# Index stage of a fused transformer kernel: eight of the sixteen heads summed on GpSimd instead of six

## The chip, the cores and the metric

One core of one Trainium2 chip runs the whole program as one launch. The metric is the device time of that launch in microseconds. A shorter time is better. A difference under 0.2% of the time (6 us) is taken as no change.

## What is computed

The program chains seven stages over 2048 tokens of width 256: a mixture of experts, attention, experts again, a feed-forward stage, the **index** stage, the sparse attention over the rows that it selected, and a feed-forward stage. The change touches the index stage alone. Its reference, cut to what matters:

```python
qi = hadamard((x @ wq_idx).reshape(B, S, Hi, Di))    # Hi = 16 heads, Di = 128
ki = hadamard(x @ wk_idx)
iw = x @ w_iw                                        # one weight for each token and head
logits = relu(einsum('bthd,bsd->bhts', qi, ki))
I = einsum('bth,bhts->bts', iw, logits)              # sum over the 16 heads
I = where(causal, I, NEG)
vals, idx = top_k(I, 32)
```

So for each query token and each key the sixteen relu results are multiplied by a weight of either sign and added up. Then the 32 largest sums of each row are searched.

## The kernel before, in words

Queries are handled in tiles of 128 tokens (partitions), tile 15 first, tile 0 last (`TILE_ORDER`). A tile `t` needs the keys 0 to 128(t+1). These are cut into **passes** of at most 1024 keys (`WIDE`): tiles 15 to 8 have two passes, tiles 7 to 0 have one, 24 in all. Ten passes are 1024 wide (the two of tile 15, the first ones of tiles 14 to 8, and tile 7's); the other fourteen have the widths 896, 768, 640, 512, 384, 256 and 128, each twice. A pass goes through the heads 0 to 15. The text calls a pass of 1024 keys wide, and the others narrow.

One head of one pass is a unit (`iunits`), and goes like this:

- TensorE makes the scores in one of four PSUM slots of two banks (`ibanks`, `IR = 4`; lines 35 to 37 are the three matmuls of a split fp32 product). `room(key)` makes it wait until the unit four places earlier has left its slot.
- ScalarE takes the relu, scaled by the absolute value of the weight (`iwa`). `relu(|w| x)` needs the sign of `w` afterwards (`iws`, which is +1 or -1).
- For a head in `VH` the relu stays in PSUM (line 1771). VectorE multiplies by the sign and adds to `Isc` in one instruction (line 1858; for head 0 lines 1861, 1864 and 1865). The PSUM slot is free when VectorE is done.
- For a head in `PH` the relu goes to one of three SBUF buffers `rlp` (`RL = 3`, line 1778), and the PSUM slot is free as soon as ScalarE is done. ScalarE then multiplies the buffer by the sign (`signed`, line 1747), and GpSimd adds the buffer to `part_sum` (line 1914 for the first two heads at once, line 1917 for the others). `PH` is (1, 3, 5, 7, 9, 11), so `VH` has ten heads, and the heads 12 to 15 and 0 are five `VH` heads in a row.

After head 15 VectorE waits for GpSimd's last sum and adds `part_sum` to `Isc` (line 1871). GpSimd has one `part_sum`, so its first instruction of the next pass waits for this addition.

VectorE also searches the previous tile: 11 steps (`topk_step`, lines 1844, 1846, 1848, each over the whole row of the tile before; tiles 3 to 0 have other steps) are spread over the units of the tile. At tiles 15, 11, 7 and 3 the four key/value products of a group of tiles and eight query products (`("q", d, pair)`) come first in the queue of every engine; ScalarE copies a query product to `qih` and VectorE makes its rest, `qil` (line 1884).

All queues are written out in program order. The semaphores are: `i_L` scores ready, `i_R` relu done, `i_sg` sign set, `i_B` GpSimd's count, `i_A` VectorE's count.

Of the kernel before, what the change touches and what calls it, by code (L numbers as in the profile page):

```python
# [9 lines left out]
ALU = mybir.AluOpType  # L10
# [29 lines left out]
def build(nc, a, out, stages=("moe0", "attn0", "moe1", "ffn0", "index1", "select1", "ffn1")):  # L40
# [13 lines left out]
    with ctx:  # L54
# [7 lines left out]
        def sb(name, shape, dt, c=None):  # L62
            return (c or ctx).enter_context(nc.sbuf_tensor(name, shape, dt))
# [70 lines left out]
        def ln_gpsimd(g, n):  # L134
            for c in range(NCH):
                ln_root(g, n, c)
# [21 lines left out]
        def ln_scalar(s, n, c):  # L158
            q = NCH * n + c
            for k in range(KD):  # L160
                s.wait_ge(ln_tr, KD * q + k + 1)
                s.copy(XTh[:, k, CH * c:CH * (c + 1)], ln_bank(c, k, n)).then_inc(ln_hi, 1)
# [23 lines left out]
        before = sb("before", [P, P], F32, moe_ctx)  # L186
# [891 lines left out]
        for kind_, u_, h_, r_ in STEPS:  # L1078
            for k_ in range({"K": 2, "P": 3, "M": u_ % NCH + 1, "R": 1, "F": 1, "G": 2}.get(kind_, 0)):
                key_ = kind_, u_, h_, r_, k_  # L1080
# [456 lines left out]
        RL = 3  # L1537
# [8 lines left out]
        iws = iw  # L1546
        Isc = sb("Isc", [P, 2, T], F32, i_ctx)
        rlp = sb("rlp", [P, RL, WIDE], F32, i_ctx)
        part_sum = sb("part_sum", [P, WIDE], F32, i_ctx)
# [17 lines left out]
                             "i_A i_k i_sg i_B i_xt").split())  # L1567
        i_kvd = [sem("i_kvd0"), sem("i_kvd1")]
        NTB = (NHI + 1 + 1) // 2
        PH = (1, 3, 5, 7, 9, 11)  # L1570
        VH = tuple(h for h in range(NHI) if h not in PH)
        IR = 4
        QP = NHI // 2

        def iunits(t):

            return [(h, lo, min(WIDE, (t + 1) * P - lo)) for lo in range(0, (t + 1) * P, WIDE) for h in range(NHI)]

        def passes(t):
            return -(-((t + 1) * P) // WIDE)  # L1580
# [7 lines left out]
        SCORED, PASSED, QUEUE = {}, {}, {}  # L1588
# [13 lines left out]
                inumber, iscored, ipassed = inumber + 1, iscored + 1, ipassed + 1  # L1602
        ITEMS = list(QUEUE)
        PER = len(VH) + (len(PH) > 0)

        def searches(t):
            return DENSE_STEPS if t < DENSE else TOPK_STEPS
# [4 lines left out]
        def counted(t, h, lo):  # L1612

            heads = PH if h in PH else VH
            return len(heads) * PASSED[t, lo] + heads.index(h)

        def added(t, h, lo):

            return PER * PASSED[t, lo] + VH.index(h) + 1

        def finished(t):

            return PER * (PASSED[t, (passes(t) - 1) * WIDE] + 1)

        def ibanks(key):
            at = 2 * (QUEUE[key] % IR)
            return ps[:, at:at + 2, :].rearrange("p b s -> p (b s)")
# [12 lines left out]
        def index_tensor(pe, n):  # L1640
# [28 lines left out]
            def room(key):  # L1669
                if QUEUE[key] >= IR:  # L1670
# [3 lines left out]
                    elif before[0] == "q":  # L1674
                        pe.wait_ge(i_ql, QP * before[1] + before[2] + 1)
                    elif before[1] in PH:
                        pe.wait_ge(i_R, SCORED[before] + 1)
# [43 lines left out]
        def index_scalar(s, n):  # L1721
            k0 = LNA[n]

            def turned(first, last):
                for m in range(first, last):
                    hs = slice(2 * m, min(2 * m + 2, NHI + 1))
                    size = (hs.stop - hs.start) * KD * DI
                    s.wait_ge(i_t, m + 1)
                    s.copy(wih[:, hs], ps[:, 4 + m % 4, 0:size]).then_inc(i_th, 1)

            s.wait_ge(i_c, 64)
            s.copy(ikv_h[:], ikv_raw[:]).then_inc(i_rh, 1)
            ln_scalar(s, k0, 0)
            ln_scalar(s, k0, 1)
            turned(0, 4)
            ln_scalar(s, k0, 2)
            turned(4, NTB)
            ln_scalar(s, k0, 3)
            for c in range(NCH):
                s.wait_ge(i_ki, c + 1)  # L1740
                s.copy(KIh[:, CH * c:CH * (c + 1)], ps[:, 2 + c % 2, :]).then_inc(i_kh, 1)
            before = None

            def signed(t, h, lo, w):
                at = rlp[:, counted(t, h, lo) % RL, 0:w]
                s.wait_ge(i_R, SCORED[t, h, lo] + 1)
                s.activation(at, at, ACT.Copy, scale=iws[:, t, h:h + 1]).then_inc(i_sg, 1)  # L1747

            for d in range(NCH):
                c = NCH - 1 - d  # L1750
                for t in reversed(range(CT * c, CT * (c + 1))):
                    p = TILES - 1 - t
                    o = ibanks(("kv", t, 0))
                    s.wait_ge(i_kv, p + 1)
                    if p >= 2:
                        s.wait_ge(i_kvd[p % 2], 16 * (p // 2))
                    s.copy(iw[:, t, :], o[:, 2 * P:KVI])
                    s.copy(kvs[:, p % 2, :], o[:, 0:2 * P]).then_inc(i_kve, 1)
                for pair in range(QP):
                    s.wait_ge(i_q, QP * d + pair + 1)  # L1760
                    if d >= 1 and pair == 0:
                        s.wait_ge(i_L, SCORED[CT * (c + 1), NHI - 1, (passes(CT * (c + 1)) - 1) * WIDE] + 1)
                    s.copy(qih[:, 2 * pair:2 * pair + 2, :].rearrange("p h t -> p (h t)"), ibanks(("q", d, pair))).then_inc(i_qh, 1)
                s.wait_ge(i_iw, 4 * (d + 1))
                for t in reversed(range(CT * c, CT * (c + 1))):
                    for h, lo, w in iunits(t):
                        key = (t, h, lo)
                        o = ibanks(key)[:, 0:w]
                        s.wait_ge(i_L, SCORED[key] + 1)
                        if h in VH:  # L1770
                            s.activation(o, o, ACT.Relu, scale=iwa[:, t, h:h + 1]).then_inc(i_R, 1)  # L1771
                            if before:
                                signed(*before)
                            before = None
                        else:
                            m = counted(t, h, lo)
                            s.wait_ge(i_B, max(m - RL + 1, 0))
                            s.activation(rlp[:, m % RL, 0:w], o, ACT.Relu, scale=iwa[:, t, h:h + 1]).then_inc(i_R, 1)  # L1778
                            before = t, h, lo, w

        def index_vector(v, n):
            k0 = LNA[n]
# [68 lines left out]
            def scores(t, h, lo, w):  # L1851
                acc = Isc[:, t % 2, lo:lo + w]
                if h in VH:
                    o = ibanks((t, h, lo))
                    v.wait_ge(i_R, SCORED[t, h, lo] + 1)
                    if h > 0:
                        v.wait_ge(i_A, added(t, h, lo) - 1)
                        i = v.scalar_tensor_tensor(out=acc, in0=o[:, 0:w], scalar=iws[:, t, h:h + 1], in1=acc,  # L1858
                                                   op0=ALU.mult, op1=ALU.add)
                    elif lo + w < (t + 1) * P:  # L1860
                        i = v.tensor_scalar(acc, o[:, 0:w], iws[:, t, h:h + 1], None, ALU.mult)
                    else:
                        if w > P:
                            v.tensor_scalar(acc[:, 0:w - P], o[:, 0:w - P], iws[:, t, h:h + 1], None, ALU.mult)
                        i = v.scalar_tensor_tensor(out=acc[:, w - P:w], in0=o[:, w - P:w], scalar=iws[:, t, h:h + 1],
                                                   in1=imask[:], op0=ALU.mult, op1=ALU.add)
                    i.then_inc(i_A, 1)
                if h == NHI - 1 and PH:
                    v.wait_ge(i_A, added(t, VH[-1], lo))
                    v.wait_ge(i_B, len(PH) * (PASSED[t, lo] + 1))  # L1870
                    v.tensor_tensor(acc, acc, part_sum[:, 0:w], ALU.add).then_inc(i_A, 1)

            for d in range(NCH):
# [30 lines left out]
        def index_gpsimd(g, n):  # L1904
            ln_gpsimd(g, LNA[n])
            for t in TILE_ORDER:
                for h, lo, w in iunits(t):
                    if h in PH[1:]:
                        m = counted(t, h, lo)
                        at = rlp[:, m % RL, 0:w]  # L1910
                        g.wait_ge(i_sg, m + 1)
                        if h == PH[1]:
                            g.wait_ge(i_A, PER * PASSED[t, lo])
                            g.tensor_tensor(part_sum[:, 0:w], rlp[:, (m - 1) % RL, 0:w], at, ALU.add).then_inc(i_B, 2)  # L1914
                        else:
                            g.wait_ge(i_B, m)
                            g.tensor_tensor(part_sum[:, 0:w], part_sum[:, 0:w], at, ALU.add).then_inc(i_B, 1)  # L1917


# [506 lines left out]
```

## Time and profile before

| what | us |
|---|---|
| median of three runs | 2947.57 (2947.53 to 2949.59) |
| the profiled execution, its own time | 2954.38 |
| its span, first to last instruction | 2952.6 |
| scoring part of the index stage within the span (tile 15's first VectorE operation to the last addition) | 1571.3 to 2150.6 |
| mean granted TensorE clock of the span | 0.946 of 2.4 GHz |

The profile counts time from the span's start. Its views name engines as PE (TensorE), DVE (VectorE), ACT (ScalarE) and POOL (GpSimd). A row of a group says line, engine, operation, output and input, shape, count, then the busy time, the mean duration of one in ns, and how long the engine sat idle just before. Durations of successive instructions of one engine can overlap a little: ScalarE's next relu starts about 0.1 us before the last one is recorded as ended, and a matmul of 512 columns is recorded as 0.39 us while the next one starts 0.23 us after it.

### The profile page before, as it was taken

How to read it: one execution, taken by the hardware profiler on the slowest of the kernel's cores; microseconds unless marked ns; L12 is line 12 of the kernel's file. 1: busy time of each engine (PE TensorE's matmuls, PEld its weight loads, DVE VectorE, ACT ScalarE, POOL GpSimd, SP SyncE). 2: the span in 40 equal slices, each digit the busy share in tenths (PEclk: the TensorE clock that was granted, in tenths of full speed). 3: DMA queues.
4: the chain of work that ended last, by engine and by line, in shares of the span. 5: the costliest groups of instructions: out<-in, count | busy, mean ns of one | idle time of the engine just before them, and what ended most of it. 6: DMA issues, size and time to landing. Idle time of an engine off the chain costs nothing. (4 is left out here: it accounts for less than half of the span.)

```text
span 2952.6 us, 42059 instructions
## 1 busy us (share of the span) xinstructions
PE 2561.3 (87%) x14687; PEld 1967.1 (67%) x14687; DVE 1816.7 (62%) x3482; ACT 1492.5 (51%) x2918; POOL 1039.1 (35%) x943
## 2 busy tenths in 40 slices
PE   4957999999999996797979889898868988888798
PEld 4845555555556554676867777676768877776587
DVE  7556865865766754645455997989835444445443
ACT  3435557457556555342227876767644433434232
POOL 2642212212202201452223432424246565657232
PEclk9978999999999996898989999999989999999899
DMA  4241000000000003223010000000033232323200
GB/s 156 85 137 50 8 9 23 17 19 19 11 23 8 11 1 110 67 80 101 29 40 4 1 6 2 1 8 1 8 108 90 83 88 85 93 79 97 89 2 29
DMA packets 70266, 138.63 MB, mean 47 GB/s; under 512 B 16816, under 2 KB 38024, under 8 KB 68912
## 3 DMA queue, kind: packets, MB, share of 16 engines
q0 software_dynamic: 26336, 73.01, 8.3%
q1 hardware_dynamic: 43728, 62.95, 6.4%
q8 instruction: 125, 2.05, 0.3%
q14 instruction: 77, 0.63, 0.1%
HBM read 114.71 MB, written 20.81 MB: 46 GB/s over the span
## 5 line engine op out<-in xcount | busy, mean ns | idle before, releaser
L1437 ACT ACTIVATE PT<-ps 128x512 f32<-128x512 f32 (+3 forms) x640 | 313.4, 534 | 283.1 <-PE ps L1190 147.2
L2260 POOL DMA_INDIRECT KV<-kv_scratch,sidx x384 | 367.9, 958 | 238.7 <-PE ps L2107 115.3
L1303 DVE TENSOR_REDUCE xn<-ps 128x1 f32<-128x512 f32 (+3 forms) x640 | 342.4, 601 | 61.4 <-PE ps L1167 45.5
L35 PE MATMUL ps<-KIh,qih 128*128 128x512 f32 (+2 forms) x640 | 250.8, 392 | 66.0 <-DVE Isc L1858 39.7
L1858 DVE SCALAR_TENSOR_TENSOR Isc<-ps,iw,Isc 128x1024 f32<-128x1024 f32 (+7 forms) x216 | 208.6, 966 | 54.5 <-ACT ps L1771 48.4
L36 PE MATMUL ps<-KIl,qih 128*128 128x512 f32 (+2 forms) x640 | 242.0, 378 | 0.0
L37 PE MATMUL ps<-KIh,qil 128*128 128x512 f32 (+2 forms) x640 | 241.8, 378 | 0.0
L2182 ACT ACTIVATE sP<-sP,snm 128x128 f32<-128x128 f32 (+2 forms) x256 | 110.4, 432 | 251.0 <-DVE snm L2245 251.0
L1187 PE MATMUL ps<-qB,KB 128*128 128x512 f32 (+2 forms) x640 | 234.1, 366 | 0.0
L1771 ACT ACTIVATE ps<-ps,iwa 128x1024 f32<-128x1024 f32 (+7 forms) x240 | 198.2, 858 | 62.6 <-PE ps L37 62.1
L35 PEld LDWEIGHTS ps<-KIh,qih 128*128 128x128 f32 x640 | 126.3, 197 | 113.0 <-issue 91.8
L1470 POOL TENSOR_TENSOR rr<-rb 128x512 f32<-128x512 f32 x64 | 82.3, 1285 | 325.7 <-DVE rb L1295 322.3
L1473 POOL TENSOR_TENSOR qB<-rr,qA 64x512 fp32r<-64x512 f32 x64 | 81.7, 1277 | 323.8 <-ACT qB L1427 323.7
L1917 POOL TENSOR_TENSOR part_sum<-part_sum,rlp 128x1024 f32<-128x1024 f32 (+7 forms) x96 | 168.4, 1755 | 61.2 <-ACT rlp L1747 61.2
L1914 POOL TENSOR_TENSOR part_sum<-rlp 128x1024 f32<-128x1024 f32 (+7 forms) x24 | 42.2, 1757 | 352.5 <-ACT rlp L1747 281.3
L858 POOL TENSOR_TENSOR fyl<-fy,fyh 128x512 fp32r<-128x512 f32 x64 | 84.4, 1318 | 215.8 <-ACT fyh L769 215.8
L1200 PE MATMUL ps<-PT,VG 128*32 128x512 f32 (+3 forms) x1280 | 150.0, 540 | 3.8 <-ACT Osb L1441 3.5
L37 PEld LDWEIGHTS ps<-KIh,qil 128*128 128x128 f32 x640 | 126.4, 197 | 20.8
L36 PEld LDWEIGHTS ps<-KIl,qih 128*128 128x128 f32 x640 | 126.8, 198 | 19.5
L1186 PE MATMUL ps<-qA,XTh 128*128 128x512 f32 (+2 forms) x320 | 133.7, 418 | 5.1 <-DMA qA<-mrow 4.9
L1186 PE MATMUL ps<-qA,XTl 128*128 128x512 f32 (+2 forms) x320 | 136.0, 425 | 0.0
L1778 ACT ACTIVATE rlp<-ps,iwa 128x1024 f32<-128x1024 f32 (+7 forms) x144 | 125.5, 872 | 19.5 <-PE ps L37 18.8
(362 smaller groups left out, 6963.3 us busy)
## 6 DMA issues: line engine op xcount, KB each, us to landing
cs<-in_rope SPq DMA_DIRECT2D x20, 512.0 KB, 4.2
ycomb<-y_rows SPq DMA_DIRECT2D x16, 512.0 KB, 5.0
w1raw<-in_w SPq DMA_DIRECT2D x14, 512.0 KB, 6.7
KV<-kv_scratch,sidx POOLq DMA_INDIRECT x384
xn_rows<-xnr SPq DMA_DIRECT2D x8, 512.0 KB, 4.9
whr<-in_whead SPq DMA_DIRECT2D x16, 256.0 KB, 2.8
w2raw<-in_w SPq DMA_DIRECT2D x14, 256.0 KB, 7.0
wir<-in_wi SPq DMA_DIRECT2D x1, 2176.0 KB, 7.9
```

Source lines behind the costliest of these rows:

```text
L35: pe.matmul(out, lhs[0], rhs[0], start=start, stop=False)
L36: pe.matmul(out, lhs[0], rhs[1], start=False, stop=False)
L37: return pe.matmul(out, lhs[1], rhs[0], start=False, stop=stop)
L1186: pe.matmul(o[:, mm_lo:CH], KA[hh][:, j * P:(j + 1) * P], qA[:, par, hh, mm_lo:CH], start=True, stop=False)
L1187: i = pe.matmul(o[:, mm_lo:CH], KB[:, j * P:(j + 1) * P], qB[:, par, hh, mm_lo:CH], start=False, stop=j < CT * c)
L1200: i = pe.matmul(ps[2 * HD * hh:2 * HD * (hh + 1), AV_BANK, lo:CH], VG[:, j, hh, :], PT[:, ROUND[u, j] % 2, hh, lo:CH], start=j == 0, stop= ...
L1303: v.tensor_reduce(mp[:, CT * h + r, k:k + 1], o[:, 0:end], AX_X, ALU.max).then_inc(a_free, 1)
L1437: s.activation(PT[:, rnd % 2, hh, lo:CH], ps[:, ST_BANKS[e % 3], lo:CH], ACT.Exp, scale=SCALE).then_inc(a_exp, 1)
L1771: s.activation(o, o, ACT.Relu, scale=iwa[:, t, h:h + 1]).then_inc(i_R, 1)
L1858: i = v.scalar_tensor_tensor(out=acc, in0=o[:, 0:w], scalar=iws[:, t, h:h + 1], in1=acc, op0=ALU.mult, op1=ALU.add)
L1917: g.tensor_tensor(part_sum[:, 0:w], part_sum[:, 0:w], at, ALU.add).then_inc(i_B, 1)
L2260: g.indirect_dma_start(KV[:, BG * (k % RB) + m, :], None, a["kv_scratch"], bass.IndirectOffsetOnAxis(sidx[:, t % 2, at:at + 1], 0)).then_i ...
```

## The change

`PH` becomes (1, 2, 4, 5, 7, 8, 10, 11), so `VH` is (0, 3, 6, 9, 12, 13, 14, 15). ScalarE still multiplies by the sign for the four heads in `SH`, (2, 5, 8, 11). For the other four (1, 4, 7, 10) GpSimd does it: for head 1 with a `tensor_scalar` that writes `part_sum`, for the others with a `tensor_scalar` in place in `rlp`, followed by the addition. There are still three `rlp` buffers, one `part_sum` and four PSUM slots. TensorE's queue has the same instructions in the same order.

```diff
-        PH = (1, 3, 5, 7, 9, 11)
+        PH = (1, 2, 4, 5, 7, 8, 10, 11)
+        SH = (2, 5, 8, 11)
...
+        PKEYS = [key_ for key_ in ITEMS if key_ in SCORED and key_[1] in PH]
...
+        def signed_by_act(t, h, lo):
+            return len(SH) * PASSED[t, lo] + SH.index(h) + 1
+
+        def summed(t, h, lo):
+
+            heads = PH[:PH.index(h) + 1]
+            return (2 * len(PH) - 1 - len(SH)) * PASSED[t, lo] + 2 * len(heads) - 1 - sum(x in SH for x in heads)
...
                         else:
+                            if before:
+                                signed(*before)
                             m = counted(t, h, lo)
-                            s.wait_ge(i_B, max(m - RL + 1, 0))
+                            if m >= RL:
+                                s.wait_ge(i_B, summed(*PKEYS[m - RL]))
                             s.activation(rlp[:, m % RL, 0:w], o, ACT.Relu, scale=iwa[:, t, h:h + 1]).then_inc(i_R, 1)
-                            before = t, h, lo, w
+                            before = (t, h, lo, w) if h in SH else None
...
-                    v.wait_ge(i_B, len(PH) * (PASSED[t, lo] + 1))
+                    v.wait_ge(i_B, summed(t, PH[-1], lo))
...
-                    if h in PH[1:]:
+                    if h in PH:
                         m = counted(t, h, lo)
-                        at = rlp[:, m % RL, 0:w]
-                        g.wait_ge(i_sg, m + 1)
-                        if h == PH[1]:
+                        at, sign = rlp[:, m % RL, 0:w], iws[:, t, h:h + 1]
+                        if h == PH[0]:
+                            g.wait_ge(i_R, SCORED[t, h, lo] + 1)
                             g.wait_ge(i_A, PER * PASSED[t, lo])
-                            g.tensor_tensor(part_sum[:, 0:w], rlp[:, (m - 1) % RL, 0:w], at, ALU.add).then_inc(i_B, 2)
+                            g.tensor_scalar(part_sum[:, 0:w], at, sign, None, ALU.mult).then_inc(i_B, 1)
                         else:
-                            g.wait_ge(i_B, m)
+                            if h in SH:
+                                g.wait_ge(i_sg, signed_by_act(t, h, lo))
+                            else:
+                                g.wait_ge(i_R, SCORED[t, h, lo] + 1)
+                                g.tensor_scalar(at, at, sign, None, ALU.mult).then_inc(i_B, 1)
+                            g.wait_ge(i_B, summed(t, h, lo) - 1)
                             g.tensor_tensor(part_sum[:, 0:w], part_sum[:, 0:w], at, ALU.add).then_inc(i_B, 1)
```

GpSimd's queue for one pass of 1024 keys, with the semaphores that each instruction waits for. Before:

```order
L1914 TENSOR_TENSOR part_sum<-rlp 128x1024 [waits i_A,i_sg]
L1917 TENSOR_TENSOR part_sum<-part_sum,rlp 128x1024 [waits i_B,i_sg] x4
```

With the change:

```order
L1927 TENSOR_SCALAR part_sum<-rlp,iw 128x1024 [waits i_A,i_R]
L1935 TENSOR_TENSOR part_sum<-part_sum,rlp 128x1024 [waits i_B,i_sg]
L1933 TENSOR_SCALAR rlp<-rlp,iw 128x1024 [waits i_R]
L1935 TENSOR_TENSOR part_sum<-part_sum,rlp 128x1024 [waits i_B]
L1935 TENSOR_TENSOR part_sum<-part_sum,rlp 128x1024 [waits i_B,i_sg]
L1933 TENSOR_SCALAR rlp<-rlp,iw 128x1024 [waits i_R]
L1935 TENSOR_TENSOR part_sum<-part_sum,rlp 128x1024 [waits i_B]
L1935 TENSOR_TENSOR part_sum<-part_sum,rlp 128x1024 [waits i_B,i_sg]
L1933 TENSOR_SCALAR rlp<-rlp,iw 128x1024 [waits i_R]
L1935 TENSOR_TENSOR part_sum<-part_sum,rlp 128x1024 [waits i_B]
L1935 TENSOR_TENSOR part_sum<-part_sum,rlp 128x1024 [waits i_B,i_sg]
```

Five additions become seven, and four multiplications by the sign are new.

VectorE's queue in the first pass of tile 14, from head 0 to the addition of `part_sum`. Before (a row with x2 or x3 is that many heads):

```order
L1861 TENSOR_SCALAR Isc<-ps,iw 128x1024
L1858 SCALAR_TENSOR_TENSOR Isc<-ps,iw,Isc 128x1024
L1844 MAX v<-Isc 128x8
L1858 SCALAR_TENSOR_TENSOR Isc<-ps,iw,Isc 128x1024
L1846 MAX_INDEX xn<-v,Isc 128x8
L1858 SCALAR_TENSOR_TENSOR Isc<-ps,iw,Isc 128x1024 x2
L1848 MATCH_REPLACE Isc<-v,Isc 128x2048
L1858 SCALAR_TENSOR_TENSOR Isc<-ps,iw,Isc 128x1024
L1844 MAX v<-Isc 128x8
L1858 SCALAR_TENSOR_TENSOR Isc<-ps,iw,Isc 128x1024 x3
L1846 MAX_INDEX xn<-v,Isc 128x8
```

With the change:

```order
L1874 TENSOR_SCALAR Isc<-ps,iw 128x1024
L1857 MAX v8<-Isc 128x8
L1871 SCALAR_TENSOR_TENSOR Isc<-ps,iw,Isc 128x1024
L1859 MAX_INDEX xn<-v8,Isc 128x8
L1871 SCALAR_TENSOR_TENSOR Isc<-ps,iw,Isc 128x1024
L1861 MATCH_REPLACE Isc<-v8,Isc 128x2048
L1871 SCALAR_TENSOR_TENSOR Isc<-ps,iw,Isc 128x1024
L1857 MAX v8<-Isc 128x8
L1871 SCALAR_TENSOR_TENSOR Isc<-ps,iw,Isc 128x1024 x3
L1859 MAX_INDEX xn<-v8,Isc 128x8
```

In both, head 15's SCALAR_TENSOR_TENSOR and the addition of `part_sum` follow. Two of the ten head operations are gone, both before head 12; the search steps stay where they were. ScalarE's queue loses two of its six sign operations of each pass, and its relu of a `PH` head now follows another one directly.

## Rows read from the trace of the kernel before

**Rows 1.** The page: span, and busy time of each engine.

```profile
span 2952.6 us, 42059 instructions
PE 2561.3 (87%) x14687; PEld 1967.1 (67%) x14687; DVE 1816.7 (62%) x3482; ACT 1492.5 (51%) x2918; POOL 1039.1 (35%) x943
```

**Rows 2.** Windows, one a pass: length, PE, PEld, DVE, ACT, POOL busy, clock, DMA.

```profile
1598.20:1622.00 23.80, 22.85 (x98) 17.76 (x97) 14.09 (x14) 22.61 (x23) 12.02 (x5) 1.00 0.00 1
1622.00:1647.90 25.90, 22.98 (x96) 17.64 (x95) 24.75 (x21) 23.54 (x24) 12.03 (x5) 0.98 0.00 1
1671.80:1699.90 28.10, 22.75 (x100) 17.73 (x98) 26.45 (x23) 23.38 (x24) 12.06 (x5) 1.00 0.00 1
1699.90:1721.50 21.60, 18.12 (x95) 14.93 (x94) 21.15 (x21) 17.20 (x21) 9.26 (x5) 1.00 0.00 1
1881.30:1908.30 27.00, 21.45 (x93) 16.69 (x91) 23.61 (x23) 22.39 (x26) 12.02 (x5) 0.97 0.00 1
1908.30:1921.40 13.10, 10.11 (x51) 8.88 (x52) 12.65 (x22) 8.55 (x20) 3.65 (x5) 0.81 0.00 1
2011.00:2036.40 25.40, 20.31 (x97) 16.80 (x96) 25.16 (x31) 20.82 (x23) 10.65 (x5) 1.00 0.00 1
```

**Rows 3.** Waits from 1570 to 2155 us: total, times, longest.

```profile
ACT ps L1771 <- PE ps L37: 62.1, 66, 3.4
DVE Isc L1858 <- ACT ps L1771: 48.4, 59, 1.8
PE ps L35 <- DVE Isc L1858: 43.2, 52, 2.2
```

**Rows 4.** Groups of VectorE, shapes apart, 1570 to 2155 us.

```profile
L1858 DVE SCALAR_TENSOR_TENSOR Isc<-ps,iw,Isc 128x1024 f32<-128x1024 f32 x90 | 115.1, 1279 | 44.4 <-ACT ps L1771 41.9
...
L1858 DVE SCALAR_TENSOR_TENSOR Isc<-ps,iw,Isc 128x896 f32<-128x896 f32 x18 | 20.5, 1138 | 0.7 <-ACT ps L1771 0.3
...
L1858 DVE SCALAR_TENSOR_TENSOR Isc<-ps,iw,Isc 128x128 f32<-128x128 f32 x18 | 6.2, 343 | 1.2 <-ACT ps L1771 0.6
```

**Rows 5.** Timeline of ScalarE in tile 8's first pass: start, duration, idle before.

```profile
1929.20 1.08 ACT L1771 ACTIVATE ps<-ps,iwa 128x1024 f32<-128x1024 f32 x1
1930.19 1.16 ACT L1747 ACTIVATE rlp<-rlp,iw 128x1024 f32<-128x1024 f32 x1
1931.24 1.12 ACT L1778 ACTIVATE rlp<-ps,iwa 128x1024 f32<-128x1024 f32 x1
1932.23 1.10 ACT L1771 ACTIVATE ps<-ps,iwa 128x1024 f32<-128x1024 f32 x1
...
1938.30 1.12 ACT L1771 ACTIVATE ps<-ps,iwa 128x1024 f32<-128x1024 f32 x1
```

**Rows 6.** Timeline of TensorE in tile 15.

```profile
1597.66 0.39 PE L37 MATMUL ps<-KIh,qil 128*128 128x512 f32 x1
1597.89 0.40 PE L35 MATMUL ps<-KIh,qih 128*128 128x512 f32 x1
```

**Rows 7.** Timeline of VectorE at the end of tile 8's first pass.

```profile
1941.50 2.67 DVE L1858 SCALAR_TENSOR_TENSOR Isc<-ps,iw,Isc 128x1024 f32<-128x1024 f32 x2 [0.76 <-ACT ps L1771]
...
1944.16 1.49 DVE L1846 FIND_INDEX8 xn<-v,Isc 128x8 uint32<-128x1280 f32 x1
1945.56 1.26 DVE L1858 SCALAR_TENSOR_TENSOR Isc<-ps,iw,Isc 128x1024 f32<-128x1024 f32 x1
1946.86 1.22 DVE L1871 TENSOR_TENSOR Isc<-Isc,part_sum 128x1024 f32<-128x1024 f32 x1
```

**Rows 8.** Groups of GpSimd's additions and ScalarE's signs, index stage.

```profile
L1917 POOL TENSOR_TENSOR part_sum<-part_sum,rlp 128x1024 f32<-128x1024 f32 x40 | 96.1, 2403 | 25.4 <-ACT rlp L1747 25.4
...
L1917 POOL TENSOR_TENSOR part_sum<-part_sum,rlp 128x896 f32<-128x896 f32 x8 | 17.0, 2130 | 4.7 <-ACT rlp L1747 4.7
...
L1747 ACT ACTIVATE rlp<-rlp,iw 128x1024 f32<-128x1024 f32 (+7 forms) x144 | 130.8, 908 | 0.0
```

**Rows 9.** Groups of other GpSimd work in the whole span.

```profile
L132 POOL TENSOR_TENSOR rstd<-veps,mhalf 128x4 f32<-128x4 f32 x24 | 27.2, 1133 | 2.0
...
L1451 POOL MEMSET tmpq<- 128x1024 f32 x1 | 1.0, 953 | 0.0
```

## The prediction

> **What bounds the kernel now.** The page [rows 1] shows only that no engine fills the span: VectorE 62%, GpSimd 35%. The change lies in the scoring part of the index stage, 579 of 2953 us, so I read that part pass by pass. In the windows [rows 2] compare each engine's busy time with the length. In the narrow passes VectorE is full: 21.15 of 21.6 us in tile 13's second pass, 12.65 of 13.1 in tile 9's, 25.16 of 25.4 in tile 6's. There, every VectorE instruction that goes is time that goes. In the wide passes nobody is full: tile 9's first has VectorE at 23.61 and ScalarE at 22.39 of 27.0 us; tile 15's second has VectorE at 14.09 and ScalarE at 22.61 of 23.8. The waits [rows 3] say the same: TensorE waits for VectorE to free a PSUM slot, VectorE waits for ScalarE, ScalarE for TensorE, each 40 to 60 us in all; no long one has GpSimd as the cause.
>
> A wide pass has two halves. In **heads 1 to 11** ScalarE sets the pace: relu, sign, relu follow each other without a gap, and two heads take 1929.20 to 1932.23, 3.03 us [rows 5], while TensorE would need 2 x 6 matmuls x 0.23 = 2.8 us [rows 6]. In **heads 12 to 15** VectorE does: in tile 8's first pass, which begins at 1921.4 [rows 2], head 12's relu starts at 1938.30, 16.9 us in [rows 5]; then VectorE has heads 13 and 14 (2.67), a search step (1.49), head 15 (1.26) and the addition of `part_sum` (1.22), until 1948.1 [rows 7]: 9.8 us from the relu's start.
>
> **The change, part by part.**
>
> *VectorE, two heads fewer in each pass.* One costs 1.279 us at 1024 keys, 1.138 at 896, 0.343 at 128 [rows 4]. The fourteen narrow passes are two of each width from 128 to 896; the duration grows evenly with the width, so the mean is (1.138 + 0.343) / 2 = 0.74 and the 28 instructions are 20.7 us. VectorE is full there, so nearly all counts; I take off 2 us for the narrow passes of tiles 3 and 4, beside query products and key/value products that TensorE sets. **-19 us.**
>
> *ScalarE, two signs fewer.* In all 144 signs are 130.8 us [rows 8], a third goes, 44 us. In the narrow passes this is hidden behind VectorE, which stays the longer: tile 13's second pass has 21.15 against 17.20 [rows 2]. In the wide passes it moves the pace of heads 1 to 11 from ScalarE to TensorE: three heads are now four ScalarE operations of 1.01 us, 4.05, against 18 matmuls, 4.2 us. Eleven heads at 1.4 instead of 1.52 are 1.3 us less, at most. The end of the pass, from head 12 on, is VectorE's and has the same instructions. In tile 8 TensorE alone would bring head 12 about 1.0 us sooner. I take 1.0 for each of the first passes of tiles 7 to 11. Tile 14's I put at 0.8, since it is only 25.9 us long. Tiles 13 and 12 are longer, because VectorE with a 2048 or 1792 wide search is nearly full there (26.45 of 28.1 [rows 2]): the two heads are 2.56 us, of which I count 2.1 and 2.5. Tile 15's two passes: nothing, see the next part. 5.0 + 0.8 + 4.6 = **-10.4 us.**
>
> *GpSimd, more work.* Before, five additions of 2.403 us, 12.0 us in a wide pass [rows 2, 8]; now seven, 16.8 us, and four multiplications. The trace has no GpSimd multiplication by a column of scalars at these widths. From below: a memset of 128x1024 takes 0.953 us [rows 9], which only writes. From above: the addition, two inputs and one output, 2.403. A multiplication reads one and writes one. Half of an addition for the one input it reads is 1.20, and it lies just above the memset; I take c = **1.25 us** and keep 0.95 to 2.4 for the range. Each instruction waits for the semaphore of the one before; the pair of line 130 and line 132 shows 2.0 us over 24 such waits [rows 9], 0.08 us. So GpSimd's round in a wide pass is 11 instructions, 4 c + 16.8 + 0.9, then VectorE's addition of 1.2 and a signal of 0.1, before the single `part_sum` is free: 4 c + 19.0 = 24.0 us. That is above the 23.8 of tile 15's second pass and below the 25.9 to 28.1 of the others [rows 2]. So tile 15 gains nothing, and the others may shrink as far as the sum above has them. At 896 keys an addition is 2.130 and the round about 21.5, just under VectorE's. One more wait is in it: ScalarE's relu into a buffer waits for the sum three `PH` heads back. Head 11's waits for head 7's: 3 c + 4 x 2.4 + 0.6 = 14.0 us after GpSimd's start, which in tile 8 is 0.9 us into the pass. Everything behind it in ScalarE's queue, heads 12 to 15, waits too, and VectorE with them. Head 11's relu would be ready about 14.5 us into the pass, so the wait is some 0.4 us. I charge **+1.5 us** for the wide passes.
>
> The Trainium skill ("GPSIMD Engine Reference", section 4.1, Engine selection) speaks against elementwise work on GpSimd: two-input operations about twice as slow as on VectorE, one-input ones roughly at line rate. The first half agrees with the trace, 2.403 against 1.22 us for an addition [rows 7, 8]. By the second half c would be near 1.0, and the sum, an estimate, some 2 us better. No run here shows that half yet.
>
> *Sum:* -19 - 10.4 + 1.5 = -28. TensorE's queue, the DMAs and every other stage are unchanged: nothing. Against the profiled execution (2954.4, which stands 6.8 above the median) that is 2926; against the median of 2947.6 it is **2919.5 us**.
>
> **The rivals.**
>
> *A. GpSimd's multiplication costs about what an addition does, and GpSimd's round becomes the bound.* For it: it is the same engine, with a fixed share for each element, and in-place work behind a semaphore. Against: one input less. With c = 2.4 the round is 28.6 us in a wide pass. The passes of before are 23.8 to 28.1 [rows 2]; over the ten I count a mean of 26.7, so ten of them lose 1.9 each, 19 us. At 896 and 768 keys the rounds would be 25.4 and 22.3, 1 us over what stands there; the other narrow passes keep their gain, about 10 us. Together +11: **2959 us**. It is slower than before from c = 2.2 up.
>
> *B. In between, c around 1.9.* The round of a wide pass is 26.6: the wide passes as a whole gain nothing, head 11's relu comes 1.9 us later, and the narrow ones give 15 to 17. **2932 us.**
>
> *C. VectorE's time does not come back in full.* The eight heads left are unevenly placed: three in heads 1 to 11, five in a row from head 12. TensorE can only be four units ahead, so what VectorE saves before head 12 may turn into waiting for ScalarE, also in passes where it is full now. Then the narrow passes give half, 10 us, and the wide ones 5 to 8: **2931 us**. Against it: the search steps are spread over all heads, and in tile 13's second pass heads 1 to 11 leave VectorE three heads and four steps of about 2 us, 11.2 us, with ScalarE at 15 operations of 0.8, 12.0, and ahead by some heads.
>
> *D. VectorE gives all of it.* Both heads gone count everywhere but in tile 15, and c is near 1.0: 48 instructions less four of tile 15, about 41 us, **2907 us**.
>
> **How the numbers follow.** Forecast (c up to 1.6, loss small) 0.57; D 0.08; C 0.13; B 0.08; A 0.11; 0.03 for a mix that ends near zero. A measurement of this kernel tells 0.2%, 6 us, from no change. Faster by more than that: forecast, D, C and nearly all of B, 0.85. Slower by more: most of A, 0.09. Within: the rest, 0.06. The range leaves out D's best end and the upper part of A: 2908 to 2942.
>
> **What would show it.** Right: a multiplication row of GpSimd at 1.0 to 1.5 us for 1024 keys; VectorE still full in the narrow passes, tile 13's second near 19.6 us instead of 21.6; wide passes of 24 to 26 us with TensorE's matmuls 0.23 apart through heads 1 to 11; GpSimd at 20 to 22 us of them. Wrong: a multiplication of 2 us and more; VectorE's addition of `part_sum` waiting for GpSimd in most passes; ScalarE's relu into `rlp` waiting for GpSimd by over a microsecond; narrow passes in which VectorE sits idle waiting for ScalarE.

## The result, and the profile after

The change makes the kernel slower: 3022.69 us median (3017.36 to 3025.36) against 2948.58 before, a ratio of 1.0243, 95% interval 1.0225 to 1.0261. The forecast was 2919.5. Even the slower rival, 2959, is far below what was measured. The two profiled executions, from which all rows come, are 63.0 us apart (3017.36 and 2954.38).

The page of the changed kernel, span and busy time of each engine, against [rows 1]:

```profile
span 3015.1 us, 42104 instructions
PE 2582.9 (86%) x14687; PEld 1977.9 (66%) x14687; DVE 1775.6 (59%) x3434; ACT 1463.0 (49%) x2870; POOL 1322.6 (44%) x1087
```

VectorE lost 41 us of work and ScalarE 29.5 (its sign operations by themselves add up to 86.0 us in place of 130.8), and GpSimd gained 283.5 us. The forecast amounts to some 169 us of new work there: the mean addition of before was 1.755 us, so 48 more are 84 us, and 96 multiplications at half of that another 84.

The windows of the changed kernel show passes that answer to those of [rows 2]: the second pass of tile 15, the first of tile 14, both of tile 13, both of tile 9, and tile 6's. The columns are the length, then PE, PEld, DVE, ACT and POOL busy, the granted clock, DMA share and GB/s:

```profile
1603.40:1633.80 30.40, 24.79 (x96) 18.76 (x96) 11.52 (x12) 21.29 (x21) 28.08 (x11) 0.94 0.00 1
1633.80:1664.20 30.40, 25.43 (x95) 19.55 (x96) 22.42 (x19) 19.41 (x19) 28.05 (x11) 0.89 0.00 0
1691.60:1724.00 32.40, 24.73 (x98) 18.82 (x97) 24.10 (x21) 21.01 (x21) 28.07 (x11) 0.93 0.00 1
1724.00:1748.20 24.20, 21.00 (x97) 17.12 (x96) 19.40 (x21) 16.73 (x20) 21.64 (x11) 0.88 0.00 1
1921.80:1953.00 31.20, 22.22 (x92) 16.77 (x90) 20.80 (x19) 20.89 (x23) 28.00 (x11) 0.93 0.00 1
1953.00:1965.00 12.00, 10.39 (x51) 9.44 (x52) 11.76 (x21) 7.84 (x18) 8.83 (x11) 0.77 0.01 2
2064.90:2093.60 28.70, 21.60 (x95) 18.05 (x96) 23.57 (x29) 17.99 (x20) 24.86 (x11) 0.94 0.00 1
```

Where 23.8, 25.9, 28.1 and 27.0 us stood, there are 30.4, 30.4, 32.4 and 31.2, and in each GpSimd works 28 us in place of 12. Of the narrow passes only the second ones of tiles 10, 9 and 8 gain (tile 9's from 13.1 to 12.0, where VectorE is still full); the last passes, of the same three widths in tiles 2, 1 and 0, are 0.4 to 1.7 us longer. The granted clock is lower than before, 0.88 to 0.94 in most of them, behind TensorE's longer waits. What this lower clock costs by itself no run here shows. Over the scoring part, adding up from one addition of `part_sum` to the next, the ten wide passes went from 318.0 to 366.3 us, and the fourteen narrow ones from 261.3 to 279.9.

Groups of GpSimd in the changed kernel, shapes apart: line, operation, tiles, shape, count, then busy us, mean ns of one, and the idle time before:

```profile
L1935 POOL TENSOR_TENSOR part_sum<-part_sum,rlp 128x1024 f32<-128x1024 f32 x70 | 167.0, 2386 | 13.5 <-ACT rlp L1757 6.3
L1933 POOL TENSOR_SCALAR rlp<-rlp,iw 128x1024 f32<-128x1024 f32 x30 | 85.6, 2852 | 2.8 <-ACT rlp L1791 2.8
...
L1927 POOL TENSOR_SCALAR part_sum<-rlp,iw 128x1024 f32<-128x1024 f32 x10 | 28.5, 2850 | 118.0 <-ACT rlp L1791 110.2 <-DVE Isc L1884 7.8
```

The multiplication takes **2.85 us**, more than the addition it was bounded by (2.403 [rows 8]). In place or into `part_sum`, it is the same.

How that reaches VectorE is to be seen in the first pass of tile 8, which begins at 1965.0. Timeline of ScalarE in the changed kernel (start, duration; in brackets the idle time before and its releaser):

```profile
1977.52 1.12 ACT L1791 ACTIVATE rlp<-ps,iwa 128x1024 f32<-128x1024 f32 x1 [1.81 <-POOL part_sum L1935]
1978.53 1.08 ACT L1781 ACTIVATE ps<-ps,iwa 128x1024 f32<-128x1024 f32 x1
...
1985.33 1.11 ACT L1791 ACTIVATE rlp<-ps,iwa 128x1024 f32<-128x1024 f32 x1 [3.64 <-POOL part_sum L1935]
1986.34 1.08 ACT L1781 ACTIVATE ps<-ps,iwa 128x1024 f32<-128x1024 f32 x1
```

and of VectorE, just after:

```profile
1987.45 1.28 DVE L1871 SCALAR_TENSOR_TENSOR Isc<-ps,iw,Isc 128x1024 f32<-128x1024 f32 x1 [5.12 <-ACT ps L1781]
...
1995.61 1.23 DVE L1884 TENSOR_TENSOR Isc<-Isc,part_sum 128x1024 f32<-128x1024 f32 x1 [0.79 <-POOL part_sum L1935]
```

Head 11's relu (1985.33) waits 3.64 us until GpSimd has emptied a buffer. Head 12's relu stands behind it and starts at 1986.34, 21.3 us into the pass, where it had been 16.9 us. VectorE, idle for 5.12 us, then does the same end of the pass as before. The whole shift of the pass is 5.1 us: 4.4 by head 12's relu, and the rest by GpSimd's own last sum, which comes out at almost the same place: VectorE's addition waits 0.79 us for it.

The waits of the changed kernel from 1570 to 2235 us (total, times, longest), against [rows 3]:

```profile
DVE Isc L1871 <- ACT ps L1781: 152.8, 79, 6.8
...
ACT rlp L1791 <- POOL part_sum L1935: 76.2, 34, 3.9
...
PE ps L35 <- DVE Isc L1871: 50.6, 65, 2.2
```

A wait that did not appear among those of before, ScalarE for GpSimd, is 76.2 us, and VectorE's wait for ScalarE has tripled from 48.4.

### The profile page after: what moved, and what is told of

Its sections match the earlier page's. It is cut to its first block and busy times, and to the rows that moved or that the text cites. A ratio compares the mean times of both kernels' runs of the same rounds, so it can differ in the third digit from the quotient of the medians.

```text
span 3015.1 us, 42104 instructions
## 1 busy us (share of the span) xinstructions
PE 2582.9 (86%) x14687; PEld 1977.9 (66%) x14687; DVE 1775.6 (59%) x3434; ACT 1463.0 (49%) x2870; POOL 1322.6 (44%) x1087
## 5 line engine op out<-in xcount | busy, mean ns | idle before, releaser
L35 PE MATMUL ps<-KIh,qih 128*128 128x512 f32 (+2 forms) x640 | 260.1, 406 | 110.6 <-DVE Isc L1871 46.2
L1935 POOL TENSOR_TENSOR part_sum<-part_sum,rlp 128x1024 f32<-128x1024 f32 (+7 forms) x168 | 293.1, 1745 | 28.3 <-ACT rlp L1757 9.9
L1871 DVE SCALAR_TENSOR_TENSOR Isc<-ps,iw,Isc 128x1024 f32<-128x1024 f32 (+7 forms) x168 | 162.5, 967 | 155.7 <-ACT ps L1781 152.8
L36 PE MATMUL ps<-KIl,qih 128*128 128x512 f32 (+2 forms) x640 | 248.8, 389 | 0.0
L37 PE MATMUL ps<-KIh,qil 128*128 128x512 f32 (+2 forms) x640 | 248.1, 388 | 0.0
L1791 ACT ACTIVATE rlp<-ps,iwa 128x1024 f32<-128x1024 f32 (+7 forms) x192 | 165.3, 867 | 143.5 <-POOL part_sum L1935 76.2
L1781 ACT ACTIVATE ps<-ps,iwa 128x1024 f32<-128x1024 f32 (+7 forms) x192 | 155.5, 842 | 37.0 <-PE ps L37 36.7
L1933 POOL TENSOR_SCALAR rlp<-rlp,iw 128x1024 f32<-128x1024 f32 (+7 forms) x72 | 151.4, 2103 | 10.1 <-ACT rlp L1791 10.0
```

The source lines that it names most:

```text
L35: pe.matmul(out, lhs[0], rhs[0], start=start, stop=False)
L36: pe.matmul(out, lhs[0], rhs[1], start=False, stop=False)
L37: return pe.matmul(out, lhs[1], rhs[0], start=False, stop=stop)
```

## The experiments

Twelve kernels ran. The medians are each beside runs of the kernel before on the same chip, whose medians were 2950.8 to 2952.4 us. Where two runs from different chips are set against each other below, each is taken by its distance from its own runs of before.

**1. Eight heads, all signs on ScalarE.** The kernel before with the change's `PH`, and a pending sign set before the next relu into a buffer:

```diff
-        PH = (1, 3, 5, 7, 9, 11)
+        PH = (1, 2, 4, 5, 7, 8, 10, 11)
...
+                            if before:
+                                signed(*before)
                             m = counted(t, h, lo)
                             s.wait_ge(i_B, max(m - RL + 1, 0))
```

> Eight heads on GpSimd as in the change, but ScalarE sets all eight signs and GpSimd only adds (7 additions a pass). Theory M (the multiplication, 2.85 us at 1024 keys, makes GpSimd's round 4 x 2.85 + 19.0 = 30.4 us and so the bound): the round falls to about 18.9 us, GpSimd no longer holds anybody, the wide passes come down from 31 us to 26 to 28 (ScalarE has 24 operations of 1.01 us), the narrow ones to VectorE's time; 2935 to 2955 us. Rival W (the uneven placing of the eight heads, with more heads for three rlp buffers, is what costs): stays at 2990 to 3020.

Measured: 2991.7 us, ratio 1.0135 (1.0115 to 1.0155). Theory M's 2935 to 2955 fails, and the value is at W's lower end. GpSimd is no longer in anybody's way (16.8 us busy in a wide pass), but the wide passes are 26.0 to 31.4 us (tiles 11 and 7, which hold the query products, aside), with ScalarE busy 24.6 to 26.0 of them. From head 1 on, before head 12's relu, ScalarE now has 11 relus and 7 signs, and in tile 8 that relu starts 19.5 us into the pass in place of 16.9; the end of the pass hangs on it. So eight heads with eight signs on ScalarE is no reference for "GpSimd without multiplications": it puts another load in its place. The waits say so: VectorE waits 127.9 us for ScalarE.

```profile
DVE Isc L1860 <- ACT ps L1771: 127.9, 84, 4.5
```

**2. Six heads, three signs on GpSimd.** The change with

```diff
-        PH = (1, 2, 4, 5, 7, 8, 10, 11)
-        SH = (2, 5, 8, 11)
+        PH = (1, 3, 5, 7, 9, 11)
+        SH = (3, 7, 11)
```

> The six heads of before on GpSimd, but GpSimd sets the sign of three of them (1, 5, 9) itself. Theory M: its round in a wide pass is 3 x 2.85 + 5 x 2.4 + 0.6 + 1.3 = 22.5 us, under the passes of before, so nothing is lost and ScalarE's three signs less give a little: 2935 to 2950 us. A rival by which the multiplication disturbs VectorE or ScalarE (shared memory access) rather than fills GpSimd: three quarters of the loss, 2990 to 3005.

Measured: 2953.0 us, ratio 1.0003 (0.9994 to 1.0013): no difference. The multiplication costs 2.854 us here too:

```profile
L1933 POOL TENSOR_SCALAR rlp<-rlp,iw 128x1024 f32<-128x1024 f32 x20 | 57.1, 2854 | 0.0
```

The rival (the multiplication disturbs the other engines) is out: 72 of them, three quarters of the change's, cost nothing in sum while GpSimd's work of 20.5 us fits in the pass. What was also expected, a small gain by ScalarE's 72 signs less, did not come.

**3. The constant 1.0 instead of the column of signs.**

```diff
-                            g.tensor_scalar(part_sum[:, 0:w], at, sign, None, ALU.mult).then_inc(i_B, 1)
+                            g.tensor_scalar(part_sum[:, 0:w], at, 1.0, None, ALU.mult).then_inc(i_B, 1)
...
-                                g.tensor_scalar(at, at, sign, None, ALU.mult).then_inc(i_B, 1)
+                                g.tensor_scalar(at, at, 1.0, None, ALU.mult).then_inc(i_B, 1)
```

> The change, but GpSimd multiplies by the constant 1.0 instead of by the column of signs, so the signs of heads 1, 4, 7 and 10 are left out. If the column of scalars is what makes the multiplication dear, its row falls to 1.0 to 1.5 us and the time to 2915 to 2930; if a GpSimd tensor_scalar costs 2.85 us by itself, both stay: 2.85 us and 3015 to 3030.

Measured: 3020.6 us, ratio 1.0235. The row hardly falls:

```profile
L1933 POOL TENSOR_SCALAR rlp<-rlp 128x1024 f32<-128x1024 f32 x30 | 83.2, 2774 | 1.5 <-ACT rlp L1791 1.5
```

This kernel leaves four signs out. The column is not the price; GpSimd's `tensor_scalar` is.

**4. The sign by a tensor_tensor.**

```diff
-                                g.tensor_scalar(at, at, sign, None, ALU.mult).then_inc(i_B, 1)
+                                g.tensor_tensor(at, at, sign.to_broadcast([P, w]), ALU.mult).then_inc(i_B, 1)
```

and the same for head 1.

> The change, but the sign is multiplied with a tensor_tensor whose second input is the sign column read again for each key. If it costs what the additions do, 2.40 us: round of 4 x 2.4 + 19.0 = 28.6 us, 1.8 us less in each wide pass and a little less in the narrow ones: 2990 to 3000 us. If the column is slow to read, 2.8 us and more: 3015 and above.

Measured: 2983.6 us, ratio 1.0098 (1.0072 to 1.0123), below what was expected, since the row is cheaper than an addition:

```profile
L1933 POOL TENSOR_TENSOR rlp<-rlp,iw 128x1024 f32<-128x1024 f32 x30 | 56.8, 1895 | 2.6 <-ACT rlp L1791 2.6
```

The same computation in another operation gives back 43 of the 74 us. But with c = 1.9 the prediction's rival B had said 2932, so something else is missing as well, and runs 5 to 7 took it to be the placing of the heads.

The trace of this run shows what is missing. Its ten wide passes are still 24 us longer in all than before, and yet VectorE's addition waits for GpSimd only in tile 15 (twice, 2.0 us in all). Tile 8's first pass begins at 1941.6; GpSimd's first two operations, ScalarE's relus of heads 11 and 12, and VectorE's end of the pass:

```profile
1942.46 1.89 POOL L1927 TENSOR_TENSOR part_sum<-rlp,iw 128x1024 f32<-128x1024 f32 x1 [3.36 <-ACT rlp L1791]
1946.30 2.41 POOL L1935 TENSOR_TENSOR part_sum<-part_sum,rlp 128x1024 f32<-128x1024 f32 x1 [1.95 <-ACT rlp L1757]
...
1960.03 1.11 ACT L1791 ACTIVATE rlp<-ps,iwa 128x1024 f32<-128x1024 f32 x1 [2.72 <-POOL part_sum L1935]
1961.04 1.08 ACT L1781 ACTIVATE ps<-ps,iwa 128x1024 f32<-128x1024 f32 x1
...
1969.56 1.23 DVE L1884 TENSOR_TENSOR Isc<-Isc,part_sum 128x1024 f32<-128x1024 f32 x1
```

Head 12's relu starts 19.4 us into the pass, 2.5 later than before; the pass is 29.2 us, 2.5 longer; and the addition of `part_sum` waits for nothing. So here the whole loss of the pass comes through the wait of head 11's relu for a buffer, and none through GpSimd's last sum. No run had a fourth buffer, which would have tested this directly.

**5 to 7. The eight heads spread over the pass.** Run 5 is the kernel of run 1 with the first line, run 6 the change and run 7 the kernel of run 4 with both:

```diff
-        PH = (1, 2, 4, 5, 7, 8, 10, 11)
+        PH = (1, 3, 5, 7, 9, 10, 12, 14)
-        SH = (2, 5, 8, 11)
+        SH = (3, 7, 10, 14)
```

> As the run with eight heads and all signs on ScalarE (2991.7 us), but the eight heads are spread: 1, 3, 5, 7, 9, 10, 12, 14, so VectorE has 0, 2, 4, 6, 8, 11, 13, 15 instead of 0, 3, 6, 9, 12, 13, 14, 15. Work of each engine is the same. Theory P (placing: VectorE idles through heads 1 to 11 and then has five heads in a row, with TensorE never more than four units ahead): 2935 to 2955 us. Rival S (ScalarE's 24 operations a pass are the bound wherever the heads lie): stays at 2980 to 2995.

> The change itself with the heads spread as 1, 3, 5, 7, 9, 10, 12, 14, ScalarE signing 3, 7, 10, 14 and GpSimd 1, 5, 9, 12 with its tensor_scalar. Both causes: GpSimd's round of 30.4 us remains the bound of the wide passes, so little of the loss comes back, and its last sum now comes after head 14: 3000 to 3025 us. If placing alone made the loss: 2950 to 2965.

> Spread heads and the cheap multiplication (tensor_tensor with the column read again, 1.895 us): GpSimd's round is 4 x 1.9 + 19.0 = 26.6 us in a wide pass, about the mean of before (26.7), ScalarE has 20 operations. If placing and multiplication were the two causes, both are gone: 2925 to 2950 us. If eight heads on GpSimd cost something else too: 2965 and above.

Measured: 2975.5 us, 1.0090 (1.0061 to 1.0119); 3063.6 us, 1.0380 (1.0363 to 1.0397); 3014.7 us, 1.0219 (1.0202 to 1.0236). Run 5 lies between its two theories, 16 us faster than run 1; 6 and 7 are 37 and 31 us slower than the same kernels with the early heads, and run 6 lies outside both of its ranges. The theory that an even placing brings the loss back falls for the kernels in which GpSimd multiplies. The waits of run 6, from 1570 to 2235 us (its scoring part ends at 2263), show what takes its place:

```profile
DVE Isc L1884 <- POOL part_sum L1935: 110.6, 20, 6.9
...
PE ps L35 <- DVE Isc L1878: 88.9, 12, 8.3
```

With a head as late as 14, GpSimd's last sum comes after VectorE is through, VectorE waits with all that is queued behind it, and then TensorE waits for head 0's slot. In run 5, whose GpSimd only adds, VectorE's wait for the sum is 33.4 us. Early heads make ScalarE wait for buffers, late heads make VectorE wait for the sum. An evenly loaded VectorE was not tested apart from this by these runs.

**8. Seven heads, 13 among them.** The kernel of run 4 with

```diff
-        PH = (1, 2, 4, 5, 7, 8, 10, 11)
-        SH = (2, 5, 8, 11)
+        PH = (1, 3, 5, 7, 9, 11, 13)
+        SH = (3, 7, 11, 13)
```

> Seven heads, 1, 3, 5, 7, 9, 11, 13; ScalarE signs 3, 7, 11 and 13, GpSimd signs 1, 5 and 9 with the cheap tensor_tensor. The head taken from VectorE lies among the five in a row that held the end of each pass. GpSimd's round: 3 x 1.9 + 6 x 2.4 + 0.7 + 1.3 = 22.1 us, below the passes. VectorE loses one head a pass (24 x 0.97 = 23 us): 2920 to 2935 us. If the one that ends last is no longer VectorE there: 2945 to 2955.

Measured: 2943.5 us, ratio 0.9970 (0.9959 to 0.9980), faster than before by a little, between the two expected ranges. The narrow passes sum to 251.1 us against 261.3, the wide ones to 321.7 against 318.0.

**9. The change without its four multiplications.** GpSimd adds the first two buffers and then the others (the signs of heads 1, 4, 7 and 10 are missing), everything else is the change:

```diff
-                            g.tensor_scalar(part_sum[:, 0:w], at, sign, None, ALU.mult).then_inc(i_B, 1)
...
-                                g.tensor_scalar(at, at, sign, None, ALU.mult).then_inc(i_B, 1)
+                            if h == PH[1]:
+                                g.tensor_tensor(part_sum[:, 0:w], rlp[:, (m - 1) % RL, 0:w], at, ALU.add).then_inc(i_B, 2)
+                                continue
```

> The change with GpSimd's four multiplications left out (the signs of heads 1, 4, 7 and 10 are missing); heads, placing, ScalarE's 20 operations and seven additions as in the change. Theory H (a wide pass is the time until head 12's relu plus some 9.8 us of VectorE work; in the change head 11's relu waits for head 7's sum, 3 c + 4 x 2.4 + 0.6 us after GpSimd's start, 18.8 us with c = 2.85): with c = 0 that wait is gone, TensorE sets heads 1 to 11, wide passes of 25 to 26.5 us, narrow ones at VectorE's time: 2912 to 2930 us. Rival P (the uneven placing costs by itself, 2960 to 2985 us whatever GpSimd does).

Measured: 2938.1 us, ratio 0.9960 (0.9941 to 0.9979). This is the run that parts the loss in two. The change is 74 us above its runs of before and this kernel 13 below its own: the multiplications cost 87 us, more than the whole loss. Whether they do it by head 11's wait, as theory H has it, or by GpSimd's whole round, this run can't tell, since it takes both away; run 4 shows head 11's wait alone at work, and in the change's tile 8 the two came out within 0.8 us of each other. But 2938 is above H's 2912 to 2930, so a part of the forecast gain is missing even where GpSimd has no multiplication.

Part of what is missing is this kernel's own. GpSimd's first instruction now takes two buffers at once and can't begin before head 2's sign is set, so it frees head 1's buffer late, and head 5's relu waits for it: 1.41 us in tile 8, 1.66 each in tiles 11 and 7, 11.7 us in ten waits.

```profile
1919.35 1.12 ACT L1791 ACTIVATE rlp<-ps,iwa 128x1024 f32<-128x1024 f32 x1 [1.41 <-POOL part_sum L1933]
```

In the timeline of VectorE in tile 5's pass (768 keys, 23.4 us before, 23.5 here) the place shows:

```profile
2032.28 1.09 DVE L1857 MAX8 v<-Isc 128x8 f32<-128x896 f32 x1
2035.08 1.02 DVE L1871 SCALAR_TENSOR_TENSOR Isc<-ps,iw,Isc 128x768 f32<-128x768 f32 x1 [1.71 <-ACT ps L1781]
...
2043.24 1.02 DVE L1871 SCALAR_TENSOR_TENSOR Isc<-ps,iw,Isc 128x768 f32<-128x768 f32 x1 [0.60 <-ACT ps L1781]
```

VectorE has done head 3 and its search steps and stands idle for 1.71 us until head 6 arrives; head 13 waits 0.60 us, because ScalarE sets head 11's sign between the relus of 12 and 13. The windows of the same kernel for that pass and for tile 13's second (21.6 us before):

```profile
1697.00:1718.20 21.20, 19.80 (x98) 16.00 (x97) 19.40 (x19) 16.39 (x20) 12.94 (x7) 0.95 0.01 1
...
2025.70:2049.20 23.50, 19.94 (x97) 16.88 (x96) 20.85 (x29) 16.38 (x20) 12.90 (x7) 0.85 0.00 1
```

VectorE is busy 19.40 of 21.2 and 20.85 of 23.5: it lost the two heads' work and got idle time for most of it.

In tile 5's pass the clock has a share in this. TensorE had stood idle for head 0's slot, and then made the scores of heads 4 to 6 at the lower of its two levels, 1.2 GHz (granted clock 0.50); the 5.6 us at the same place of the pass before had 0.70:

```profile
2028.22 0.77 PE L35 MATMUL ps<-KIh,qih 128*128 128x512 f32 x1 [2.22 <-DVE Isc L1878]
```

The windows, first of this run, then of the kernel before:

```profile
2028.20:2033.80 5.60, 5.58 (x17) 4.74 (x18) 5.11 (x7) 1.80 (x2) 3.39 (x2) 0.50 0.00 0
2038.90:2044.50 5.60, 5.58 (x22) 4.80 (x23) 5.57 (x8) 3.24 (x4) 1.84 (x1) 0.70 0.02 3
```

How much of the 1.71 us is the placing and how much the clock is not shown. From 1571 to 2135 us the mean granted clock is 0.96 in both kernels.

**10. The same with later heads.** The kernel of run 9, without multiplications, with

```diff
-        PH = (1, 2, 4, 5, 7, 8, 10, 11)
-        SH = (2, 5, 8, 11)
+        PH = (1, 3, 5, 6, 8, 10, 11, 13)
+        SH = (3, 6, 10, 13)
```

> As the run before, without multiplications, with heads 1, 3, 5, 6, 8, 10, 11, 13 on GpSimd (ScalarE signs 3, 6, 10, 13; the signs of the others are missing), so only 12, 14, 15 and 0 stand at the end of a pass on VectorE. Theory H: the end of a wide pass is one head (1.28 us) shorter, unless VectorE waits for GpSimd's sum of head 13: 2905 to 2930 us. If late heads are what hurt in the spread runs (VectorE's addition waits for GpSimd's last sum): 2935 to 2960.

Measured: 2937.7 us, ratio 0.9966 (0.9952 to 0.9981): the same as run 9, in the second range and not in theory H's. The reason that was given for the second range is not what the trace shows: VectorE's addition waits only 5.7 us in all for GpSimd's last sum. One head fewer at the end of the pass brings nothing in sum; in exchange ScalarE waits for buffers again:

```profile
ACT rlp L1791 <- POOL part_sum L1933: 27.1, 21, 1.7
```

**11. Seven heads, signs on ScalarE.** The kernel before with

```diff
-        PH = (1, 3, 5, 7, 9, 11)
+        PH = (1, 3, 5, 7, 9, 11, 13)
```

> Seven heads, 1, 3, 5, 7, 9, 11, 13, all seven signs on ScalarE, so 23 of its operations a pass. Theory H: head 12's relu is as late as before (six signs ahead of it, as before), the end is one head shorter, narrow passes gain VectorE's one head: 2930 to 2945 us. If GpSimd's signing is what made the seven heads of the earlier run (2943.5 us) faster than before: 2950 to 2965.

Measured: 2940.9 us, ratio 0.9969 (0.9959 to 0.9980), as theory H has it. It is as fast as run 8, whose GpSimd sets three signs: moving these three signs to GpSimd is worth nothing either way, moving the one head is.

**12. Seven heads without a late one.** The kernel of run 8 with

```diff
-        PH = (1, 3, 5, 7, 9, 11, 13)
-        SH = (3, 7, 11, 13)
+        PH = (1, 3, 5, 7, 9, 11, 12)
+        SH = (3, 7, 11, 12)
```

> Seven heads, 1, 3, 5, 7, 9, 11, 12, GpSimd signing 1, 5 and 9 by tensor_tensor, ScalarE 3, 7, 11, 12. Against 1, 3, 5, 7, 9, 11, 13 (2943.5 us, where VectorE's addition waited 18.7 us for GpSimd's last sum) the last sum comes one head sooner: that wait mostly goes: 2925 to 2940 us. If it does not set the pace: 2940 to 2950.

Measured: 2952.7 us, ratio 1.0004 (0.9993 to 1.0015): 11 us slower than run 8, where up to 18 us faster had been expected, and outside both ranges. The wait of VectorE's addition for GpSimd in run 8 was this:

```profile
DVE Isc L1884 <- POOL part_sum L1935: 18.7, 15, 2.4
```

In run 12 it is 8.8 us, so it did shrink, but VectorE waits 63.5 us for ScalarE instead of 50.3. So that wait did not set the pace. Why head 12 is a worse choice than head 13 was not followed further.

## Why the prediction was wrong

**The change to GpSimd's round: the step that failed, by its size.** "From above: the addition, two inputs and one output, 2.403": this upper bound was an argument (one input fewer cannot cost more), not a measurement, and it is false on this engine. The multiplication takes 2.85 us, 1.6 more than the 1.25 taken. At this c the formulas behind it come close. The round, 4 c + 19.0, gives 30.4 us at 2.85; tile 15's second and tile 14's first pass are 30.4, the first passes of tiles 13 to 8 without query products 31.3 to 32.4. The wait of head 11's relu, 3 c + 4 x 2.4 + 0.6 after GpSimd's start, gives 18.8; in tile 8 GpSimd started at 0.9 and the relu at 20.3 us, 19.4 later. The 0.6 too little are in ScalarE's order: head 2's sign comes only after head 3's relu, so GpSimd's first addition waits 0.97 us.

**The same formula had a second fault, which c = 2.85 nearly hides.** GpSimd's first addition needs head 2's sign, and so starts 4.7 us into tile 8's first pass in the change and in run 4 alike. A first multiplication of 2.85 us fills most of the time until then; in run 4, with 1.9, GpSimd stands idle for 1.95 before the addition, and head 11's relu comes 17.6 us after GpSimd's start where the formula gives 15.9. From the rows of both runs: GpSimd's first addition ends at 7.1, then come two multiplications, three additions and their waits (7.5), so head 11's relu is at 14.6 + 2 c, which gives 20.3 and 18.4, as measured. With the forecast's own c of 1.25 this is an estimate of 17.1, not 14.9, and head 12's relu would be at 18.1, later than the 16.9 of before, where a gain of 1.0 was counted. No run has a multiplication of that length, but the time lies 13 us under before without any (run 9) and 31 above it at 1.9 (run 4). So "the wait is some 0.4 us" and the charge of 1.5 us were too small by themselves, and the forecast of -28 would probably have failed with the right c too. Rival B, 2932, missed run 4's 2984 by the same step.

**Rival A** had the mechanism, the bound and the direction, but c = 2.4 as its end and a chance of 0.11. Its sum of 2959 would be short even with the right c: wide passes of 30.4 to 32.4 in place of 28.6 (and the longer ones of tiles 11 and 7) give 48 us instead of 19, and the narrow passes, which it let keep about 10 us, lost 18.6. In tile 12's second pass, 640 keys, GpSimd is busy for 18.4 us and VectorE for 17.5, so GpSimd is the longer one there too.

**The skill's rule.** The Trainium skill ("GPSIMD Engine Reference", section 4.1, Engine selection) has one-input operations roughly at line rate. For `tensor_scalar` the trace does not agree: 2.85 us for 1024 keys with a column, 2.77 with a constant (run 3), where VectorE's own one (line 1861 of the kernel before, out of PSUM) takes 1.28, and GpSimd's memset 0.953 [rows 9]. The measurement decides. The general warning of the same page, that elementwise arithmetic belongs on VectorE, stands. The trace agrees: 2.40 against 1.22 us for an addition [rows 7, 8].

**VectorE's -19 us.** Run 9 measures this term, with GpSimd out of the way: the narrow passes sum to 252.4 against 261.3, -8.9. "VectorE is full there, so nearly all counts" failed: it is full with ten heads in that order, not with eight of which three lie in heads 1 to 11. That is rival C as it was written, half in the narrow passes. C said 2931 for it, and run 9 has 2938. That the placing makes this loss is C's argument; no run has eight heads, no multiplications and an even placing with no wait for the sum, and in tile 5 the low clock had a share.

**The wide passes' -10.4 us.** Run 9: 313.3 against 318.0, -4.7. The direction and the mechanism hold in tiles 8 to 10, where head 12's relu comes 0.3 to 0.9 us sooner: tile 8's at 16.6 in place of 16.9, and the pass is 26.3 in place of 26.7. The gain per pass is 0.4 to 0.9 us there, and not 1.0. Tiles 11 and 7, 1.0 each in the forecast, became 0.3 longer, and tile 13, where 2.1 was counted, 0.5. Run 9 is no clean measure of this term, since its own buffer waits (11.7 us in all) are in it; how much of the missing 5.7 us they make stays open.

**What held.** With GpSimd at 20.5 us of work in a wide pass (run 2) nothing is lost, as its round formula says. The stages ahead did not move: from 0 to 1570 us TensorE is busy 1372.3 us before and 1374.6 after. Behind the scoring part the profiled execution of the change is 4.5 us shorter (797.5 against 802.0), which no run explains.

In sum: without the multiplications the change gains about 13 us of the 28 forecast (run 9, its own buffer waits included), and the four multiplications of a pass cost 87.

Two kernels that leave nothing out beat both: seven heads with 13 among them, 2940.9 us with ScalarE's signs (run 11) and 2943.5 (run 8), 0.3% below before.

## What to carry to other kernels

An operation that the trace has never shown on an engine has no upper bound from its neighbours; when it will be queued 96 times on an engine with little slack, measure it by itself first, or give "dearer than anything here" a chance of its own. Work taken from a full engine comes back only as far as the next engine delivers evenly: look at where in the round the operations lie, and at which one the tail hangs, not at sums. An engine fed through few buffers passes its delay on to everything queued behind the waiting writer; write out which instruction frees each buffer and what that instruction itself waits for, in queue order. An engine's busy time against the length of the pass did not show it: in run 4 GpSimd was busy 24.2 of 29.2 us.

## What the runs showed of the hardware

On GpSimd, fp32, 128 x 1024: `tensor_scalar` with a column 2.85 us, with a constant 2.77, `tensor_tensor` add 2.40, and `tensor_tensor` whose second input is one column read for every element 1.895. So a scale by a column of scalars is a third cheaper as a `tensor_tensor` with a broadcast second input than as the operation made for it. VectorE's durations were not touched by GpSimd's load: 1.279 us a head before, 1.28 in the changed kernel's rows.
